# A spiking transformer block on one NeuronCore: LIF operations split in two in the fill, and a new order of the drain

## The reference, cut to what matters

```python
R, K, V = x @ Wr.T, x @ Wk.T, x @ Wv.T            # 256 features each
for t: r, k, v = lif(R_t), lif(K_t), lif(V_t)     # spikes, 0 or 1
       h = h * 0.9 + k * v;  y_t = r * h
x1 = layernorm(x + y @ Wo.T)                      # LN1
s1 = lif_scan(x1 @ W1.T + b1)                     # 1024 features
ffn = lif_scan(s1 @ W2.T + b2)                    # 256 features
a  = layernorm(x1 + ffn)                          # LN2
x3 = layernorm(x + a)                             # LN3
g  = softmax(x3 @ Wg + bg); best 2 of 8 experts, weights renormalised
out = layernorm(x3 + sum(g_e * (x3 @ We[e] + be[e])))   # final
```

## Time and profile before

| | |
|---|---|
| time, three runs | median 977.22 us (976.9 to 978.69) |
| profiled execution | 978.42 us, of which its span, first to last instruction, 976.6 |
| TensorE matmuls | busy 930.1 us, 95% of the span |
| VectorE | busy 917.0 us, 94% |
| ScalarE, GpSimd | 611.3 us (63%), 572.1 us (59%) |
| mean granted clock of TensorE | 0.988 of full |

### The profile page before, as it was taken

One profiled execution on the slowest core, in us unless ns is written; L12 is line 12 of the kernel. 1 busy time (PEld: TensorE's weight loads), 2 busy tenths in 40 slices (PEclk: granted clock), 3 DMA queues, 4 the chain that ended last, 5 costly groups with the idle time before them and its releaser, 6 DMA issues.

```text
span 976.6 us, 20766 instructions
## 1 busy us (share of the span) xinstructions
PE 930.1 (95%) x6586; PEld 864.8 (89%) x6586; DVE 917.0 (94%) x3680; ACT 611.3 (63%) x1392; POOL 572.1 (59%) x731
## 2 busy tenths in 40 slices
PE   8988889999999999999999999999999999999975
PEld 7878789999999999999999999999999999788764
DVE  7899998999999999999999999999999999989875
ACT  6665455667666666676666667766666676555542
POOL 1221226766666776666677766666776666664542
PEclk9999999999999999999999999999999999999988
DMA  8643224445656555456555544665555455547754
GB/s 280 156 87 66 55 55 87 103 104 109 120 122 126 110 109 106 99 122 119 120 120 108 109 104 103 120 127 123 112 106 110 97 119 108 105 92 137 139 103 97
DMA packets 59437, 109.71 MB, mean 112 GB/s; under 512 B 6592, under 2 KB 6592, under 8 KB 59328
## 3 DMA queue, kind: packets, MB, share of 16 engines
q0 software_dynamic: 37728, 68.71, 41.1%
q1 hardware_dynamic: 16992, 31.30, 9.7%
q10 hardware_dynamic: 4608, 8.39, 2.2%
HBM read 31.29 MB, written 8.39 MB: 41 GB/s over the span
## 4 chain that ended last, share of the span: by engine, by line
PE 72%; DVE 17%; issue 3%; DMA 3%; ACT 3%; POOL 2%; SPq 0%; POOLq 0%; DVEq 0%; ACTq 0%
PE ps_e L420 29%; PE ps_proj L420 10%; PE ps_proj L510 10%; PE ps_proj L495 9%; PE ps_proj L518 5%; DVE U L984 4%; PE ps_attn L420 3%; DVE V L991 3%; PE ps_zx L474 2%; DMA odd_sum<-term 2%; DVE stats L1063 2%; DVE h L1033 1%; PE ps_attn L474 1%; DVE s L1456 1%; POOL s L1528 1%
## 5 line engine op out<-in xcount | busy, mean ns | idle before, releaser
L984 DVE SCALAR_TENSOR_TENSOR U<-V,U 128x256 f32<-128x256 f32 (+4 forms) x576 | 228.3, 396 | 3.9 <-ACT U L725 1.9
L991 DVE SCALAR_TENSOR_TENSOR V<-U 128x256 f32<-128x256 f32 (+4 forms) x576 | 224.6, 390 | 1.9
L420 PE MATMUL ps_e<-we_hi,x_hi 128*128 128x512 f32 (+1 forms) x618 | 220.6, 357 | 0.1
L420 PE MATMUL ps_e<-we_lo,x_hi 128*128 128x512 f32 (+1 forms) x618 | 215.7, 349 | 0.0
L420 PE MATMUL ps_e<-we_hi,x_lo 128*128 128x512 f32 (+1 forms) x618 | 215.1, 348 | 0.0
L1514 POOL TENSOR_SCALAR veps<-mv 128x2 f32<-128x2 f32 x128 | 47.0, 368 | 271.4 <-DVE mv L1069 269.4
L1528 POOL TENSOR_SCALAR s<-U 128x256 fp32r<-128x256 f32 x208 | 192.7, 982 | 16.3 <-DVE V L991 16.3
L764 ACT ACTIVATE term<-ps_e,gate 128x256 f32<-128x256 f32 x361 | 155.4, 475 | 40.9 <-PE ps_e L420 40.7
L725 ACT ACTIVATE U<-ps_proj,cst 128x256 f32<-128x256 f32 x320 | 135.2, 479 | 68.9 <-PE ps_proj L518 60.4
L510 PE MATMUL ps_proj<-x_hi,w_hi 128*128 128x256 f32 x512 | 133.2, 282 | 0.9 <-ACT x_hi L743 0.9
L710 ACT ACTIVATE U<-ps_proj 128x512 f32<-128x512 f32 x96 | 57.2, 597 | 121.1 <-PE ps_proj L420 121.1
(11 more groups left out here) (125 smaller groups left out, 2359.5 us busy)
## 6 DMA issues: line engine op xcount, KB each, us to landing
odd_sum<-term POOLq DMA_DIRECT2D x94, 256.0 KB, 3.3
acc<-term POOLq DMA_DIRECT2D x93, 256.0 KB, 3.7
xt<-x_T SPq DMA_DIRECT2D x33, 256.0 KB, 3.0
xa<-x_tok SPq DMA_DIRECT2D x32, 256.0 KB, 3.2
xb<-cst SPq DMA_DIRECT2D x32, 256.0 KB, 2.3
xb<-x_tok POOLq DMA_DIRECT2D x32, 256.0 KB, 6.1
xt<-x_hi POOLq DMA_DIRECT2D x31, 256.0 KB, 4.3
out<-res ACTq DMA_DIRECT2D x31, 256.0 KB, 2.0
```

Of the source, the lines that this page charges most:

```text
L420: mm = pe.matmul(dst, lhs, rhs, start=(i == 0), stop=(i == n - 1))
L984: v.scalar_tensor_tensor(out=U[:, s, t, c0:c1], in0=V[:, c0:c1], scalar=0.5, in1=U[:, s, t, c0:c1], op0=ALU.mult, op1=ALU.add).then_inc(do ...
L991: v.scalar_tensor_tensor(out=V[:, c0:c1], in0=u, scalar=THRESHOLD, in1=u, op0=ALU.is_lt, op1=ALU.mult).then_inc(done, 1)
```

## The change

In beats 2 to 6 each LIF operation becomes two, one on the 96 columns of r, k, v (semaphore `lif`) and one on the remaining ones (semaphore `lif_h`): membrane, membrane, slot, reset, reset, slot. The eight spike operations leave slot -1 for slots 0, 1, 2, 3, 3, 5, 6 and 8. LN1 moves from slots 1, 2, 3, 4, 7 to 4, 5, 6, 7, 10, and x1_lo by one or two slots (beat 5 keeps 17). wo_lo moves in beat 3 from slot 31 to 16. Twelve matmuls without use are put ahead of beat 4's first work. In the drain the last beat before the tail has a table of its own (LAST_S), expert 0 of the next beat goes ahead of z_T on TensorE, expert part 5 goes ahead of the gates' transposes, VectorE's tail takes the LIF operations of beat 35 one at a time between the others, and fin 1 to 3 go behind x3_lo and z there. ScalarE's normalisation and store of beat 35 moves into beat 36, behind two expert reads; GpSimd's order changes by one place.

```diff
-FILL = dict(z_sum=-1, y=(-1,) * 5, spikes_h1=-1, fin_sum=-1,
+FILL = dict(z_sum=-1, y=(-1,) * 5, spikes_h1=(0, 1, 2, 3, 3, 5, 6, 8), fin_sum=-1,
             gate=(4, 5, 6, 7, 8, 10, 10, 11, 11, 12, 24, 26), add_e0=(13, 14),
-            ln1_sum=1, ln1_stats=(2, 3), ln1_aggr=4, ln1_norm=7, x1_low=17,
+            ln1_sum=4, ln1_stats=(5, 6), ln1_aggr=7, ln1_norm=10, x1_low=17,
...
-X1_LOW = {1: 23, 3: 19, 4: 19, 6: 15}
+X1_LOW = {1: 23, 2: 18, 3: 21, 4: 21, 6: 17}
+LAST_S = dict(DRAIN, ln3_shift=18, fin_add=22, fin_stats=23, fin_aggr=24, x3_low=26)
...
+    def split_lif(self):
+        return FIRST_SPLIT <= self.k < FIRST_STEADY      # 2 to 6
...
-                expert(b, 4)
+                for part in (4, 5):
+                    expert(b, part)
                 gates_T(b)
                 x3_T(b)
-                for part in (5, 6):
-                    expert(b, part)
+                expert(b, 6)
                 biases(b)
                 after = Beat(b.k + 1)
+                expert0(after)
                 if after.has(LAG_Z):
                     z_T(after)
-                expert0(after)
...
+                if b.k == LAG_S + 1:
+                    pe.wait_ge(x1_ready, b.value(DK, LAG_Y))
+                    bridge(ps_attn[:, 0, :], BRIDGE_Y)
...
                     if b.late and after.tail:
+                        expert0(after)
                         z_T(after)
-                        expert0(after)
...
+                if b.k == FIRST_TAIL + 1:
+                    leave(Beat(FIRST_TAIL))
                 if b.has(LAG_Z):
-                    for part in (2, 3):
+                    for part in (2, 3, 4):
                         read_expert(b, part)
                     norm_x3(b)
                 if b.has(LAG_M):
                     turned_gates(b)
                 if b.has(LAG_Z):
                     read_x3(b)
-                    for part in (4, 5, 6):
+                    for part in (5, 6):
                         read_expert(b, part)
-                leave(b)
+                if b.k > FIRST_TAIL:
+                    leave(b)
...
+            def tail(b):
+                halves = iter([half for t in range(STEPS) for half in ((0, t), (1, t))] if b.lif() else [])
+                membrane_reset = lif_part(b, *lif_columns(b), lif, b.value(2 * STEPS, 0)) if b.lif() else ()
+                def lif_next(n):
+                    for which, t in itertools.islice(halves, n):
+                        membrane_reset[which](t)
+                if b.k == FIRST_TAIL:
+                    fin_stage(b, 0)
+                lif_next(1)
+                for step in range(4):
+                    gate_stage(b, step)
+                    lif_next(1)
+                dve.wait_ge(zT_done, b.value(1, LAG_Z, 1))
+                for j in range(TILES):
+                    bn_stats(1, j, ps_zx[:, j, :], ln2_steps)
+                    lif_next(1)
+                bn_aggr(b, 1, ln2_steps, LN2_STEPS, LAG_Z, 2)
+                gate_stage(b, 4)
+                after(ln2_steps, LN2_STEPS, LAG_Z, b, 4)
+                for j in range(TILES):
+                    ln2_scale(b, j)
+                if b.k > FIRST_TAIL:
+                    fin_stage(Beat(b.k - 1), 4)
+                    fin_stage(b, 0)
+                for step in range(5, 10):
+                    gate_stage(b, step)
+                    lif_next(1)
...
+                for j in range(TILES):
+                    add_e0(b, j)
+                    lif_next(1)
+                for step in (10, 11):
                     gate_stage(b, step)
+                    lif_next(1)
                 mean_shift(b, 2, ln3_steps, LAG_Z)
+                lif_next(2 * STEPS)
+                if not b.lif():
+                    for step in (1, 2, 3):
+                        fin_stage(b, step)
                 x3_low(b)
                 if Beat(b.k + 1).has(LAG_Z):
                     next_sum(b)
+                if b.lif():
+                    for step in (1, 2, 3):
+                        fin_stage(b, step)
+                else:
+                    fin_stage(b, 4)
...
-                for step in range(4):
-                    gate_stage(b, step)
                 fin_stage(b, 0)
-                for step in range(4, 10):
+                for step in range(10):
                     gate_stage(b, step)
                 add_e0(b, 0)
                 add_e0(b, 1)
                 gate_stage(b, 10)
                 gate_stage(b, 11)
-                add_expert(b, 2)
+                for fill in (2, 3):
+                    add_expert(b, fill)
                 fin_stage(b, 1)
                 fin_stage(b, 2)
-                add_expert(b, 3)
+                add_expert(b, 4)
                 fin_stage(b, 3)
-                add_expert(b, 4)
-                fin_stage(b, 4)
...
                 add_expert(b, 5)
+                fin_stage(b, 4)
...
+                    parts = [lif_part(b, c0, COL_H1 if b.split_lif else c1, lif, b.value(2 * STEPS, 0))]
+                    if b.split_lif:
+                        parts.append(lif_part(b, COL_H1, c1, lif_h, b.value(2 * STEPS, FIRST_SPLIT)))
                     for t in range(STEPS):
-                        membrane(t)
+                        for membrane, _ in parts:
+                            membrane(t)
                         side(b, 2 * t)
-                        reset(t)
+                        for _, reset in parts:
+                            reset(t)
                         side(b, 2 * t + 1)
...
-                reciprocal_std(b, 3, fin_steps, FIN_STEPS, LAG_F, 6)
                 if b.has(LAG_Z):
                     add_odd(b, LAG_M, 3)
                     add_even(b, LAG_M, 4)
+                if b.k == FIRST_TAIL:
+                    add_odd(b, LAG_M, 5)
+                reciprocal_std(b, 3, fin_steps, FIN_STEPS, LAG_F, 6)
+                if b.has(LAG_Z) and b.k > FIRST_TAIL:
                     add_odd(b, LAG_M, 5)
```

More of the change, by code:

```diff
@@ L19 @@
+import itertools
 from contextlib import ExitStack
@@ L63 @@
 FIRST_TAIL = CHUNKS + LAG_S
+FIRST_SPLIT = 2
 C_B1, C_B2, C_G1, C_BE1 = 0, FK, FK + DK, FK + 2 * DK
@@ L83 @@
 BRIDGE_ATTN, BRIDGE_T, BRIDGE_W1 = 46, 4, 8
+BRIDGE_Y = 12
 TERM_SLOTS = E - 2
@@ L106 @@
 FIRST_Y = dict(FILL, ln1_sum=6, ln1_stats=(7, 8), ln1_aggr=9, ln1_norm=13)
-X1_LOW = {1: 23, 3: 19, 4: 19, 6: 15}
-DRAIN = dict(z_sum=-1, y=(-1,) * 5, spikes_h1=-1, fin_sum=9,
+X1_LOW = {1: 23, 2: 18, 3: 21, 4: 21, 6: 17}
+DRAIN = dict(z_sum=-1, y=(-1,) * 5, spikes_h1=(-1,) * FK, fin_sum=9,
              gate=(-1, -1, -1, -1, 0, 1, 2, 3, 4, 4, 6, 7), add_e0=(11, 12),
@@ L140, in ahead @@
         return self.late and Beat(self.k - 1).late and self.has(LAG_S)
+    @property
+    def split_lif(self):
+        return FIRST_SPLIT <= self.k < FIRST_STEADY
     @property
@@ L285, in build @@
         proj_filled, proj_read = sem("proj_filled"), sem("proj_read")
-        lif = sem("lif")
+        lif, lif_h = sem("lif"), sem("lif_h")
         state_steps = sem("state_steps")
@@ L971, in spikes_view, with lif_part @@
                 return U[:, slot, :, tile * B:(tile + tiles) * B]
-            def lif_part(b, c0, c1):
+            def lif_part(b, c0, c1, done, before):
                 s = b.k % 2
-                done = lif
-                before = b.value(2 * STEPS, 0)
                 def membrane(t):
@@ L1277, in ln2_finish @@
                 dve.wait_ge(xb_ready, b.value(16, LAG_Z, 16))
[L1278 to L1279 removed]
+                for j in range(TILES):
+                    ln2_add(b, j)
                 after(ln2_steps, LN2_STEPS, LAG_Z, b, 8)
[L1281 to L1282 removed]
+                for j in range(TILES):
+                    bn_stats(2, j, w[:, j, :], ln3_steps)
                 bn_aggr(b, 2, ln3_steps, LN3_STEPS, LAG_Z, 2)
[L1285 to L1314 removed]
+                for j in range(TILES):
+                    add_e0(b, j)
+                    lif_next(1)
+                for step in (10, 11):
+                    gate_stage(b, step)
+                    lif_next(1)
                 mean_shift(b, 2, ln3_steps, LAG_Z)
[L1316 to L1319 removed]
+                lif_next(2 * STEPS)
+                if not b.lif():
+                    for step in (1, 2, 3):
+                        fin_stage(b, step)
                 x3_low(b)
@@ L1360, in side @@
                 state_in_lif(b, slot)
-                at = STEADY if not b.edge else FIRST_Y if b.k == LAG_Y else FILL if b.early else DRAIN
+                at = STEADY if not b.edge else FIRST_Y if b.k == LAG_Y else FILL if b.early else LAST_S if Beat(b.k + 1).tail else DRAIN
                 if b.has(LAG_Z):
@@ L1372, in side @@
                     v.tensor_tensor(y_lo[:], y, y_hi[:].bitcast(F32), ALU.subtract).then_inc(y_lo_ready, 1)
-                if b.k == LAG_S and slot == 2 * STEPS - 1:
+                if b.k == LAG_S and slot == STEPS:
                     dve.wait_ge(wo_hi_ready, 1)
```

(21 more changed lines are left out.)

36 lines of the change are left out of this document (1 added, 35 removed).

## The result

The changed kernel takes 985.3 us (median of 4 runs, 984.7 to 986.7) where the kernel before took 978.0 in the same session (4 runs): ratio 1.007, interval 1.0057 to 1.0083. The forecast was 975.7 with 970 to 981; the time lies outside it. The profiled execution has a span of 982.9 us and 984.7 us in all, against 976.6 and 978.42: 6.3 us more.

What follows compares the result with a forecast made beforehand. VectorE was taken to bound the fill to about 141 us, TensorE the 26 steady beats, with a drain behind. Drain -9.5 plus fill +8.0 gave -1.5 on 977.2: 975.7 us, range 970 to 981.

Steps and rivals of the forecast that it cites:

- The cost of two operations for one: Fill, VectorE, beats 2 to 6: each split LIF pair costs +0.075 us, 12.0 us added over 160 operations.
- Rival D: Fill: each half costs its whole duration, +0.15 us for each of 160 operations, +24, giving 991.7 us; chance 0.02.
- the rule as the prediction read it: VectorE: the next operation starts only when the pipeline is empty, so no gap to regain and each half costs its whole duration.
- With two chains in turn no LIF operation finds its predecessor unfinished: Fill, VectorE, beats 2 to 6: alternating halves remove the dependency gaps, 5.8 us taken off.
- The larger one is TensorE's loop in beat 5: Fill: beat 5's late LN1 shift delays z_T of beat 6, so VectorE waits +1.8 us at LN2's statistics.
- Rival A: Fill: VectorE's sum alone counts, +5 us without TensorE's loop, giving 972.7 us; chance 0.24.
- rival B: Beats 3 to 6: x1 chain starves TensorE, half clock lengthens W2 and W1, hand-over 10.5 us late, 979.7 us; chance 0.14.
- the prediction's own sign: Whole kernel: prediction wrong if the fill is under +4 or over +10.5 us, or the drain gains less than 6.5.
- The drain: End of the kernel: TensorE's 5.71 us hole goes and the last waits shrink; -9.5 us, bounds -6.5 to -11.5.
- The give-back through ScalarE: Beat 36: ScalarE's store and extra expert read make x3 1.9 us late, cutting the 8.7 gain to 7.1 at beat 37's expert 0.
- The last part: Last beat: two expert sums stand ahead of the odd_sum DMA wait and that chain ends sooner; 2.4 us more gained.
- the two forecast waits: Fill, VectorE: about 0.5 us for x1 at beat 2's x1_lo and 1.8 us for ps_zx in beat 6.

Runs made afterwards that it cites:

- The gap experiment: Changed kernel with one dependent membrane-reset pair made on purpose behind LN1's aggregate in each of beats 2 to 6; 982.0 us, ratio 1.0034.
- the shift experiment: Changed kernel with LN1's shift three slots later in beats 2 to 6 and beat 6's gate steps 5 to 9 at slots 14 and 15; 991.8 us.
- the bridge: Changed kernel with 20 matmuls without a use ahead of the x1 transpose in beats 4 to 6; 983.3 us, ratio 1.0055.
- the gate experiment: Changed kernel with gate steps 5 to 9 of beat 6 at slots 14 and 15 instead of 10 to 12; 985.9 us, ratio 1.0075.
- the drain alone: Kernel before with only the new drain: whole LIF operations, old slots, no added matmuls in beat 4, wo_lo at slot 31; 969.7 us, ratio 0.9901.
- the three together: Changed kernel with the dependent pair, the 20 matmuls ahead of the x1 transpose and the later gate steps of beat 6; 979.6 us, ratio 1.0013.
- e1: Changed kernel with every LIF operation whole again, moved slots, added matmuls and new drain kept; 976.3 us, ratio 0.9975.

## Why the prediction was wrong, step by step

**The cost of two operations for one: right.** In the changed kernel a pair of halves of 224 columns starts every 0.37 us (49.90, 50.27, 50.64) for a forecast of 0.375, and VectorE's own added time to the hand-over is 6.5 us for 6.7. Rival D is out, and with it the rule as the prediction read it: two halves do not cost two durations. The section of the Trainium skill that it cites ("VectorE: DVE Perf Modes", The DRAIN you can't avoid) goes on to say that a next operation that is not held starts earlier, which the prediction left out and the rows bear out.

**"With two chains in turn no LIF operation finds its predecessor unfinished": true, and that was the harm.** The step counted the dependency gaps as pure loss for VectorE, 5.8 us to be regained. They were also the moments at which GpSimd got its operation through. This is the step that failed first: the sum had no term for it, and it made 2.8 us of VectorE's waits (three stops at LN1's shift), in the LN1 chain that the whole fill hangs on, and GpSimd's additions 1.0 to 1.5 us longer. The gap experiment gives 3.3 us back with one gap a beat (1.4 of them in the fill of the profiles); the shift experiment shows that waiting longer gives GpSimd nothing. The Trainium skill ("SBUF — State Buffer", SBUF: two separate sides) has the rule that I should have weighed: GpSimd and VectorE share a port pair, and it names VectorE operations with two SBUF inputs against GpSimd operations that read SBUF; the one that starts first keeps it for its whole instruction. The runs agree on who is shut out, and add what the section does not say: GpSimd is shut out over a row of back-to-back VectorE instructions, 3.0 us of them, not over one.

**"The larger one is TensorE's loop in beat 5": the mechanism right, its extent wrong.** VectorE's wait for ps_zx in beat 6 was forecast at 1.8 and is 1.3. But the same loop, through W2, W1 and ScalarE's U, closes in beats 3 to 5 as well. Rival A's argument, that TensorE had 1 to 2.5 us of idle time in those beats, was mine too; the time from LN1's shift to the next LIF had no such slack. In the changed kernel it shows only as 0.9 us, because VectorE is late by then for the other reason; without halves it is 4.4 us (0.9, 2.6, 0.9), and the order by itself costs 7 us, where the forecast gave it 2.3 us of waits (0.5 and 1.8) and 1.0 for x1_lo's later slots, and took 1.2 off. Part of the 7 us can be LN3's stop in beat 5, 1.3 to 1.4 us, which the prediction did not list. How the 7 us divide is read from the waits; the run shows only their sum.

**The half clock: named, in rival B, and worth about 2 us** by the bridge, at the edge of the noise. B had the place and the direction; it put the hand-over at +10.5, and by the prediction's own sign a fill beyond that makes it wrong.

**ScalarE's exponential in beat 6: missed.** LN1's shift and gate step 5 met in slot 10, and ScalarE's queue has the normalisation (1.09 us) ahead of the exponential. 1.7 us of VectorE's time, but 0 of the kernel's by the gate experiment.

**The drain: -9.5 forecast, -7.5 in the profiles.** Up to z_T of beat 36 the forecast holds to 0.3 us (947.0 for 946.76). The give-back through ScalarE was forecast (x3 of beat 36 late), but TensorE then idles 2.23 us and goes on at half clock: its transposes and expert 6 take 1.5 us more than at full clock. Expert 0 of beat 37 is done 5.5 us sooner instead of 7.1 (the step's own terms, 8.7 less 1.9, make 6.8). The last part gives 2.4 as forecast: 8.8 us from the last expert to the end for 11.2. By the runs the drain alone is worth 0.99% (0.84 to 1.14), 8 to 11 us, so the 9.5 stands as well as it can be measured; single executions with the new drain are 6.8 to 9.7 us shorter from z_T of beat 33 to the end.

So of the error in the two profiles, 6.0 us are the fill's, waits of +7.1 for +1.1, and 2.0 the drain's. By the medians it is nearly all the fill's: the changed kernel lies 1.7 points, some 16 us, above the drain alone, where the forecast had 8. The 6.0 us of waits are 2.8 at LN1's shift, 1.3 at LN3's, 1.7 for the exponential and 0.9 for U, less 0.7 by which the two forecast waits were shorter (0.3 for 0.5 and 1.3 for 1.8). What I could not have seen in the rows of before is that a 0.03 us gap carries another engine; what I could have is that GpSimd stood in the chain at all, at 0.26 and 0.87 us between the aggregate and the shift. I never listed it.

**Open.** In beats 5 and 6 of the changed kernel four additions end with no recorded stop of VectorE near them. LN2's end at 111.01 and 139.14, both 0.17 us after VectorE began LN1's sum (110.84, 138.97), which takes one of its two inputs from PSUM; the same distance, 0.15 to 0.17, stands in the runs with one gap, the later shift, the bridge, the later gate and the three together. That fits the rule of two SBUF inputs, but no run changed that alone. LN1's end at 116.24 and 145.11, 0.18 and 0.19 after LN2's scaled addition began (116.06, 144.92); that one reads SBUF twice, and why it lets GpSimd in is not known. Nor was it tried which VectorE operations hold GpSimd off: the rows in question mix one and two SBUF inputs. And the last part of the drain, from z_T of beat 36 to the end, varies between the profiles of kernels that have its order in common: 36.1 us and half clock in the changed kernel, 34.5 and full clock in e1, 37.2 and half clock in the drain alone.

## What to carry to other kernels

Before closing the gaps of a busy VectorE, list who else lives in them: here a small GpSimd operation on the critical chain needed VectorE to pause, if only for 0.03 us, and giving it more slots did not help. Order the work so that one dependent pair stands right behind what GpSimd waits for. And when an operation of a pipelined loop moves later by three slots, follow the loop through every engine in every beat, not only in the beat where it is already tight: idle time of TensorE is no slack of the loop.
